# Attention as fp16 hi/lo products on four 64x64 tiles, and the graph phase's transposes and distances summed in PSUM

## The reference

```python
W = adj * adj
x = layernorm(x + einsum('bnf,nm->bmf', x, W) + bias)

z_l, z_g, v = x @ W_lang.T, x @ W_grav.T, x @ W_V.T
zn  = z_l / max(norm(z_l), 1e-8)
A_l = max(zn @ zn.T, 0) * not_eye
d2  = max(sq + sq.T - 2 * z_g @ z_g.T, 0)          # sq: squared norms of the rows of z_g
A_g = exp(-d2 / (2 * sigma**2)) * not_eye
K   = w * rownorm(A_l * adj) + (1 - w) * rownorm(A_g * adj)
x = layernorm(x + (K @ v) @ W_O.T)
```

## Time and profile before

| | before |
|---|---|
| median of 3 executions | 627.45 us (626.82 to 627.95) |
| span of the profiled execution | 625.0 us |
| TensorE busy | 614.2 us |
| vector engine busy | 444.2 us |
| ACT busy | 242.7 us |
| POOL busy | 155.5 us |

### The profile page before, as it was taken

How to read it: one execution, slowest core, us unless ns; L and a number is a source line. 1 busy time by engine, 2 the same in 40 slices (tenths; PEclk the granted TensorE clock), 3 DMA queues, 4 the chain that set the end, 5 groups by cost and what they waited for, 6 DMA issues and landing times.

```text
span 625.0 us, 11961 instructions
## 1 busy us (share of the span) xinstructions
PE 614.2 (98%) x4468; PEld 315.0 (50%) x4468; DVE 444.2 (71%) x940; ACT 242.7 (39%) x413; POOL 155.5 (25%) x159
## 2 busy tenths in 40 slices
PE   9999999999999999999999999999999999999994
PEld 6543545454454545454454545445454545545452
DVE  1759486877868586876868687786858788686564
ACT  2345224333443424434432433344342443443333
POOL 1002205032231403123230503223140312323021
PEclk9999999999999999999999999999999999999999
DMA  8722203434123342423223342312334242302103
GB/s 269 244 44 87 51 1 68 136 53 125 52 62 116 64 134 60 141 42 87 90 50 134 67 134 55 120 51 58 119 67 134 59 143 42 92 17 51 69 2 135
DMA packets 89392, 55.05 MB, mean 88 GB/s; under 512 B 70816, under 2 KB 70816, under 8 KB 89376
## 3 DMA queue, kind: packets, MB, share of 16 engines
q1 hardware_dynamic: 19744, 38.05, 17.9%
q10 hardware_dynamic: 69632, 16.79, 13.4%
HBM read 21.27 MB, written 16.78 MB: 61 GB/s over the span
## 4 chain that ended last, share of the span: by engine, by line
PE 96%; DVE 2%; ACT 1%; POOL 0%; issue 0%; POOLq 0%; ACTq 0%; DVEq 0%
PE proj L359 31%; PE proj L375 27%; PE front L339 9%; PE ps_t L389 7%; PE front L429 4%; PE ps_k L429 4%; PE ps_t L400 3%; PE ps_v L409 2%; PE proj L499 2%; PE proj L529 2%; PE ps_v L416 2%; PE ps_t L499 1%; PE ps_k L329 1%; DVE p_lo L736 1%; PE ps_t L529 1%; DVE y L709 0%
## 5 line engine op out<-in xcount | busy, mean ns | idle before, releaser
L557 ACT ACTIVATE p_hi<-proj 128x512 f16<-128x512 f32 x128 | 75.9, 593 | 118.2 <-PE proj L359 117.7
L736 DVE TENSOR_TENSOR p_lo<-proj,p_hi 128x512 f16<-128x512 f32 x128 | 86.0, 688 | 20.9 <-ACT p_hi L557 17.9
L375 PE MATMUL proj<-m_hi,ht_hi 128*128 128x512 f16 x256 | 97.2, 380 | 0.7 <-DVE p_lo L736 0.7
L375 PE MATMUL proj<-m_hi,ht_lo 128*128 128x512 f16 x256 | 97.0, 379 | 0.0
L375 PE MATMUL proj<-m_lo,ht_hi 128*128 128x512 f16 x256 | 97.0, 379 | 0.0
L1026 POOL TENSOR_TENSOR ve<-mv,eps_ln 128x4 f32<-128x4 f32 x31 | 6.6, 212 | 307.7 <-DVE mv L718 211.5
L562 ACT ACTIVATE u<-proj 128x512 f32<-128x512 f32 x64 | 37.9, 592 | 82.7 <-PE proj L375 82.5
L543 ACT ACTIVATE h_hi<-h 128x512 f16<-128x512 f32 x64 | 36.5, 619 | 69.0 <-DVE h L726 69.0
L1065 POOL TENSOR_TENSOR h_lo<-h,h_hi 128x512 f16<-128x512 f32 x30 | 41.5, 1403 | 84.4 <-ACT h_hi L543 84.4
L359 PE MATMUL proj<-ht_hi,l_grav_hi 128*128 128x512 f16 x160 | 60.6, 379 | 0.6 <-DVE p_lo L736 0.6
L359 PE MATMUL proj<-ht_hi,l_lang_hi 128*128 128x512 f16 x160 | 60.8, 380 | 0.0
(11 more groups left out here) (166 smaller groups left out, 1051.8 us busy)
## 6 DMA issues: line engine op xcount, KB each, us to landing
x_in<-in_x SPq DMA_DIRECT2D x16, 1024.0 KB, 7.1
out<-o SPq DMA_DIRECT2D x15, 1024.0 KB, 5.0
w_raw_lang<-in_L_gnn_W_lang SPq DMA_DIRECT2D x4, 256.0 KB, 3.1
o<-in_L_gnn_W_O SPq DMA_DIRECT2D x1, 1024.0 KB, 10.2
w_raw_grav<-in_L_gnn_W_grav SPq DMA_DIRECT2D x4, 256.0 KB, 10.1
u<-in_L_gnn_W_V SPq DMA_DIRECT2D x1, 1024.0 KB, 12.0
ht_hi<-h_hi ACTq DMA_TRANSPOSE x64, 2.4
ht_lo<-h_lo ACTq DMA_TRANSPOSE x64, 2.5
```

Of the source, the lines that this page charges most:

```text
L375: mm = pe.matmul(proj[j % 3][:, :], a[g.parity][:, k, p * P:(p + 1) * P], b[:, k, :], start=(n == 0), stop=(n == len(passes) - 1))
L557: act.activation(p_hi[:, j % 4, :, j // 4, :], by_batch(proj[j % 3]), ACT.Copy).then_inc(phi_ready, 1)
L736: dve.tensor_tensor(p_lo[:, j % 4, :, j // 4, :], by_batch(proj[j % 3]), p_hi[:, j % 4, :, j // 4, :], ALU.subtract).then_inc(plo_ready, 1)
```

## The change

- values(g, p) writes each output half with a 64-column product of its own, and takes batches in another order: output half q of value tile p holds batch rows from pair p // 2 * 2 + q, half p % 2.
- u and kt become fp16 hi and lo parts. ACT copies the hi part (u_high, kt_high), the vector engine subtracts for the lo part (u_low, kt_low). kt loses its zero blocks.
- attend is 12 products of 64 rows by 64 columns by 512 for each two pairs, so 24 in all; the wait for all of it stands ahead of the last product of project(g, 2). The fourth output goes to ps_t instead of ps_k.
- symmetrise adds T^T for the lang half alone, onto T in PSUM. The grav half's distances come out of spread and 8 transposes added on it in ps_v (r_sb, w_spread; the mask is part of w_spread, and the scale of T is gone from t_copy). The vector engine's sums and distances go, `shifted` comes; ACT gets `rectify`.
- residual becomes scalar_tensor_tensor with a scale; the last group's residual is scaled by ident_ku.

The diff at its core, first TensorE:

```diff
-            def project(g, j, first):
+            def project(g, j, first, attended=None):
...
-                        pe.wait_ge(u_ready, g.prev().count(4, j + 2))
+                        pe.wait_ge(ulo_ready, g.prev().count(4, j + 2))
...
                 for n, (k, a, b) in enumerate(passes):
+                    if attended and n == len(passes) - 1:
+                        attend_waits(*attended)
                     mm = pe.matmul(proj[j % 3][:, :], a[s][:, blk(k, c), :], b[g.parity][:, k, :],
...
             def values(g, p, first=False):
...
-                    mm = pe.matmul(proj[j % 3][:, :], a[g.parity][:, k, p * P:(p + 1) * P], b[:, k, :],
-                                   start=(n == 0), stop=(n == len(passes) - 1))
+                    for q in range(2):
+                        rows = (p // 2 * 2 + q) * P + p % 2 * N
+                        mm = pe.matmul(proj[j % 3][q * N:(q + 1) * N, :], a[g.parity][:, k, rows:rows + N], b[:, k, :],
+                                       start=(n == 0), stop=(n == len(passes) - 1))
...
             def symmetrise(g):
                 pe.wait_ge(t_ready, g.count(1, 1))
                 for b in range(GB):
-                    for half, eye in ((L, eye_l), (GR, eye_g)):
-                        mm = pe.matmul(ps_t[half, b * N:(b + 1) * N], t_sb[:, b * N:(b + 1) * N],
-                                       eye[:, :], start=True, stop=True)
+                    mm = pe.matmul(ps_t[L, b * N:(b + 1) * N], t_sb[:, b * N:(b + 1) * N],
+                                   eye_l[:, :], start=False, stop=True, skip_group_check=True)
...
             def spread(g, first):
-                pe.wait_ge(v_ready, g.count(1, 1))
+                pe.wait_ge(shifted_ready, g.count(1, 1))
+                pe.wait_ge(r_ready, g.count(1, 1))
...
-                pe.matmul(ps_v[:, :], ones_lg[:, :], v_diag[:, :], start=True, stop=True).then_inc(dj_done, 1)
+                pe.matmul(ps_v[:, :], w_spread[:, :], r_sb[:, :],
+                          start=True, stop=True, skip_group_check=True).then_inc(spread_done, 1)
+                for b in range(GB):
+                    mm = pe.matmul(ps_v[GR, b * N:(b + 1) * N], r_sb[:, b * N:(b + 1) * N],
+                                   eye_g[:, :], start=False, stop=True, skip_group_check=True)
+                mm.then_inc(d2_done, 1)
...
             def kernel_t(g):
-                    p, q = b // 2, b % 2
+                    p, q = b // 4 * 2 + b % 2, b // 2 % 2
...
+            def attend_waits(g, nxt):
+                pe.wait_ge(ktlo_ready, g.count(1, 1))
+                pe.wait_ge(ulo_ready, g.count(4, 4))
+                if nxt:
+                    pe.wait_ge(y_ready, nxt.count(4, 4))
+
+            def attend(g, a, banks, on_residual=()):
+                passes = ((kt_hi, u_hi), (kt_hi, u_lo), (kt_lo, u_hi))
+                for n, (kt, u) in enumerate(passes):
+                    for q in range(2):
+                        half = slice(q * N, (q + 1) * N)
+                        for side in range(2):
+                            mm = pe.matmul(banks[2 * a + q][side * N:(side + 1) * N, :], kt[half, 2 * a + side, :],
+                                           u[half, 2 * a + side, :], start=(n == 0 and 2 * a + q not in on_residual),
+                                           stop=(n == len(passes) - 1))
+                mm.then_inc(ku_done, 1)
...
-                project(g, 2, first)
+                project(g, 2, first, (before, nxt) if has_prev else None)
                 if has_prev:
-                    for p in range(PAIRS):
-                        attend(before, p, nxt)
+                    for a in range(2):
+                        attend(before, a, ku_bank)
...
+            pe.matmul(ps_v[L, 0:N], mask[:, :], eye_l[:, :], start=True, stop=True).then_inc(mask_turned, 1)
```

The vector engine (ACT's kt_high is one 128x256 copy for two of 64x256; POOL has one pow less):

```diff
+            def u_low(g, p):
+                dve.wait_ge(uhi_ready, g.count(4, p + 1))
+                dve.tensor_tensor(u_lo[:, p, :], proj[(8 + p) % 3][:, :], u_hi[:, p, :],
+                                  ALU.subtract).then_inc(ulo_ready, 1)
+
+            def kt_low(g):
+                dve.wait_ge(kthi_ready, g.count(1, 1))
+                dve.tensor_tensor(kt_lo[:, :, :], ps_v[:, 0:PAIRS * N].rearrange("p (a n) -> p a n", a=PAIRS),
+                                  kt_hi[:, :, :], ALU.subtract).then_inc(ktlo_ready, 1)
...
             def residual(g, p, first):
-                dve.wait_ge(ku_done, g.count(4, p + 1))
+                dve.wait_ge(ku_done, g.count(2, p // 2 + 1))
...
-                dve.tensor_tensor(o[:, p, :], ku_bank[p][:, :], h[g.parity][:, p, :], ALU.add).then_inc(sum_ready, 1)
+                dve.scalar_tensor_tensor(out=o[:, p, :], in0=ku_bank[p][:, :], scalar=ku_scale[:, 0:1],
+                                         in1=h[g.parity][:, p, :], op0=ALU.mult, op1=ALU.add).then_inc(sum_ready, 1)
...
             def back(g):
-                similarities(g)
+                u_low(g, 3)
                 gravities(g)
                 row_factors(g, None)
                 scale_rows(g)
+                kt_low(g)
...
             def iteration(g, has_prev, has_next):
...
                 if has_prev:
-                    similarities(before)
+                    u_low(before, 3)
                     gravities(before)
...
                 p_low(g, 1)
+                if has_prev:
+                    kt_low(before)
...
                     for p in range(PAIRS):
                         out_stats(before, p)
+                    if has_next:
+                        u_low(g, 0)
                     out_moments(before)
                     out_shift(before)
...
                 diagonals(g)
+                shifted(g)
+                if first or not has_next:
+                    u_low(g, 0)
+                u_low(g, 1)
                 diagonal_matrices(g)
-                sums(g)
-                distances(g)
+                similarities(g)
+                u_low(g, 2)
```

More of the change, by code:

```diff
@@ L391, in gram @@
                                        t[g.parity][:, c, b * N:(b + 1) * N],
-                                       start=(n == 0), stop=(n == len(passes) - 1))
+                                       start=(b == 0 and n == 0), stop=(n == len(passes) - 1),
+                                       skip_group_check=True)
                 mm.then_inc(gram_done, 1)
@@ L418, in kernel_t, with last_residual @@
                 mm.then_inc(kt_done, 1)
-            def attend(g, p, mixed):
-                if mixed and p in (1, 2):
-                    pe.wait_ge(y_ready, mixed.count(4, p + 2))
-                if p == 0:
[L425 to L431, removed]
+            def attend_waits(g, nxt):
[13 more added lines that the diff above has]
+                mm.then_inc(ku_done, 1)
+            def last_residual(g, p):
+                if p == 0:
+                    pe.wait_ge(last_ready, 2)
                 if p < 2:
@@ L617, in iteration @@
                 if has_prev:
-                    kt_copy(before)
+                    kt_high(before)
                 p_high(g, 2, first)
@@ L656, in iteration @@
                 if not has_next:
+                    rectify(g)
                     exponent(g)
-                u_copy(g, 2)
+                u_high(g, 2)
                 if has_prev:
@@ L661, in iteration @@
                 if has_next:
-                    exponent(g)
+                    rectify(g)
+                    exponent(g, first)
                 if has_prev:
                     normalise(before, (3,))
-                u_copy(g, 3)
+                u_high(g, 3)
             for k in range(DC):
@@ L770, in similarities @@
+                dve.wait_ge(rr_ready, g.count(1, 1))
+                dve.tensor_tensor(by_batch(r_sb, 0, N), over_batches(eye2, 0, N), over_columns(rr, 0, N),
+                                  ALU.mult).then_inc(r_ready, 1)
             def similarities(g):
-                dve.wait_ge(mr_ready, g.count(1, 1))
-                dve.scalar_tensor_tensor(out=a_sb[L, :], in0=s_sb[L, :], scalar=0.0, in1=w_sb[L, :],
-                                         op0=ALU.max, op1=ALU.mult).then_inc(a_ready, 1)
+                dve.wait_ge(relu_ready, g.count(1, 1))
@@ L799, in row_factors @@
                 dve.wait_ge(deg_ready, g.count(5, 4))
-                dve.scalar_tensor_tensor(out=cfac[:, :], in0=dinv[:, :], scalar=wv_scale[:, 0:1], in1=rr[:, :],
+                dve.scalar_tensor_tensor(out=cfac[:, :], in0=dinv[:, :], scalar=kt_scale[:, 0:1], in1=rr[:, :],
                                          op0=ALU.mult, op1=ALU.mult).then_inc(deg_ready, 1)
@@ L871, in back @@
                 dve.wait_ge(o_moved, g.prev().count(16, 32))
-                dve.wait_ge(ku_done, g.count(4, 4))
-                dve.tensor_tensor(o[:, 3, :], last_ku_bank[3][:, :], h[g.parity][:, 3, :], ALU.add).then_inc(sum_ready, 1)
+                dve.wait_ge(ku_done, g.count(2, 2))
```

(3 more changed lines are left out.)

178 lines of the change are left out of this document (89 added, 89 removed).

## The result

The changed kernel takes 660.23 us (median of 4 runs, 659.15 to 661.17) against 627.7 (4 runs, 626.82 to 628.09): 1.0521 times as long, interval 1.0506 to 1.0536. The profiled span is 657.8 us, at a mean granted clock of 0.994. Forecast were 660.3 and a span of 657.8.

A forecast was written before the change was run, and what follows sets the result against it. TensorE's instruction order was taken to bound the kernel. Span 625.0 + 24.6 (14 middle groups) + 2.5 (setup, group 0) + 5.7 (group 15, tail) = 657.8, plus 2.45 to the median: 660.3 us, range 648 to 672, chance 0.62.

The forecast's parts named there:

- TensorE's own need: TensorE's work in one middle group without waits: 35.4 us, a sum of changes of -0.30.
- rival A: In attend, row halves don't overlap, so it takes 12 slots: 670 us; chance 0.08.
- The changes of mode: Going into or out of 64-column tiles on TensorE: six a group at about 0.125 us, +0.50 a group.
- First stall: Before the sixth product of project(g, 2), TensorE waits for kt_low, delayed by u_low(before, 3): 0.92 us.
- Second stall: Before project(g, 6), TensorE waits for p_low(3), no longer covered by the longer attend: 1.10 us (0.86 to 1.5).
- Period: Length of one middle group, stalls included: 37.50 us, +1.76, times 14 groups.
- The ends: Setup and group 0 together +2.5 us; group 15 and the tail +5.7 us.
- The sum: Whole kernel: the span with middle groups and ends added, plus 2.45 from span to median: 660.3 us.
- B: In values, 64-column loads don't hide, so a pair costs 0.06 us more: 706 us; chance 0.05, unpaired case included.
- C: Middle groups have only the first stall: 645 us; chance 0.17, with the case between C and D.
- D: The u_low subtractions never reach TensorE's path, so both stalls and the ends' waits go: 624 us; chance 0.08.
- nothing is bought back: After the first stall all of TensorE is delayed, as the next group's start is counted from values 3 again.

The follow-up runs named there:

- e4: The kernel before with only its values made of pairs of 64-column products, all else as it was: 637.04 us, 1.0139.
- e12: Changed kernel with e7's tail, attend one projection later, and the Gram matrices' copy, diagonals and inverse norms taken earlier: 629.57 us, 1.0032.
- e2: Changed kernel with p_low(3) ahead of norm_rows and the copies of h, ScalarE's order to suit: 670.79 us, 1.0684.
- e8: e7 with p_high(3) first and both copies of h one step later on ScalarE and the vector engine: 654.36 us, 1.0424.
- e7: Changed kernel with gravities ahead of u_low(before, 3), and u_low(1), u_low(2), u_low(3) later in the last group and tail: 646.02 us, 1.0288.

## Why the prediction was right

- **TensorE's own need, 35.4 forecast**: 35.47. The attention came as priced, 1.51 us for 1.54, so row halves do overlap and rival A is out. The changes of mode did not: the way out of the column pairs took 0.23 before the spread and 0.29 behind values 3, where 0.125 stood. Against that symmetrise took 0.78 (333.97 to 334.75) for 0.93, and kernel_t 0.76 (350.37 to 351.13) for 0.84.
- **First stall, 0.92**: 0.85. Several errors of my terms met. The copy of values 3 starts 0.40 behind the product's slot, not 0.20, since column pairs carry a tail: in this trace a copy starts 0.21 behind pairs recorded 0.38 long, 0.35 behind 0.52 and 0.40 behind 0.58, as here. So gravities start at 343.76, 1.75 behind the slot, for the 1.43 of the text. Against that the vector engine needs 8.77 from there to kt_low (352.53), not 9.03, and TensorE arrives 10.22 behind the slot, not 10.02, through the slower way out of the values. It starts 0.14 behind kt_low's end (352.94), not 0.06. These are +0.32, -0.26, -0.20 and +0.08, which come to the difference of 0.07 within rounding.

```profile
341.79 0.58 PE L387 MATMUL proj<-m_hi,ht_lo 128*64 128x512 f16 x2
...
342.41 0.60 ACT L591 ACTIVATE uv<-proj 128x512 f16<-128x512 f32 x1 [1.07 <-PE proj L387]
```

- **Second stall, 1.10**: 0.97 by the bracket, 1.13 start to start (359.79 + 0.22 to 361.14). The residuals run at 0.66 from start to start, the value taken.
- **Period, 37.50**: 37.45, of which the stalls are 1.98 for the 2.02 forecast.
- **The ends, +8.2**: 32.8 - 23.9 = 8.9. Group 15's spread waits 2.06 for r, which stands behind u_low(1) (forecast 2.1), and in the tail gravities stand behind u_low(3), so that kernel_t waits 3.50 for ks:

```profile
631.75 0.69 DVE L769 TENSOR_TENSOR uv<-proj,uv 128x512 f16<-128x512 f32 x1 [2.62 <-ACT uv L591]
632.36 0.67 DVE L796 TENSOR_TENSOR r_sb<-eye,rr 64x512 f32<-64x512 f32 x1
...
633.14 1.10 PE L422 MATMUL ps_v<-r_sb,w_spread 128*128 128x512 f32 x2 [2.06 <-issue]
...
641.16 0.69 DVE L769 TENSOR_TENSOR uv<-proj,uv 128x512 f16<-128x512 f32 x1 [1.90 <-ACT uv L591]
641.88 0.69 DVE L808 SCALAR_TENSOR_TENSOR a_sb<-e_sb,mask 64x512 f32<-64x512 f32 x1
...
645.05 0.73 PE L434 MATMUL ps_v<-eye,ks_sb 128*64 128x64 f32 x16 [3.50 <-DVE ks_sb L835]
```

- **The sum, 660.3**: 660.23. The mechanism and its places are as written down, but the last 0.1 us is luck: the middle groups took 0.7 less than forecast and the ends 0.7 more. The 2.45 from span to median fitted as well (2.43), though the profiled execution itself took 659.64.
- **Rivals.** B fell by e4. By the Trainium skill ("TensorEngine Tiling (Array Packing)", Restrictions and Gotchas) column tiles lose the fast load; here no time shows for it. In the changed kernel the fp16 loads of 64 columns last 110 ns each (98 for 128 columns before), not the 138 that B was priced with. Two of them are 0.22, about one slot, so the unchanged step does not tell whether the two loads run side by side. C and D fell by the list of waits. D's 624 stood for no stall anywhere; that kernel could be built only by another order (e12), and takes 629.57.

What "nothing is bought back" hid: the two stalls and the order at the ends, 31 us, are a matter of order alone, on TensorE and in the queues that feed it (660.2 to 629.6 at the same arithmetic).

## What to carry to other kernels

Where one engine is busy in all of the span, a cheaper form of its work helps only if the copies that feed it have slack at the place where they are awaited; the shortened work was also their cover. Price the stall by walking the other engines' queues in order, and try to put the consumer one stage later before giving up the idea. Moving one copy alone to take its wait away can cost more than the wait (e2, e8): look at what stands behind it in every queue that it shares. And run the parts of a change apart: here one part was worth 2.1% and the other took it back.

## What the runs showed of the hardware

- Four 64x64 tiles run side by side: six steps of 0.22 for 24 fp16 products of 512 columns.
- A change between 128- and 64-column tiles costs about 0.15 us (e4: 0.62 for four). In the changed kernel the way out took 0.10, 0.23 and 0.29, behind column pairs recorded 0.38, 0.52 and 0.58 long.
- Two subtractions with operands in SBUF, on the vector engine and on GpSimd, lengthen the one that starts second: the vector engine's from 0.70 to 1.4 to 1.6 (e8, e2), or GpSimd's from 1.16 to 1.60 (the changed kernel). The low part of a projection, which reads PSUM, kept 0.69 beside it: in the changed kernel two of them take 1.29 from 361.63, while GpSimd's second copy of h runs.
- At the end TensorE idled for 3.5 us before the kernel's products, and its clock was granted at 0.50, the lower of its two levels (1.2 GHz), over the last attention; steps were 0.43 in place of 0.22. In e7, where TensorE does not idle ahead of kernel_t, the same products run at a granted 1.00 and 0.22 a step. The changed kernel:

```profile
646.70:649.10 2.40, 2.39 (x24) 0.93 (x24) 0.84 (x2) 0.00 (x0) 0.00 (x0) 0.50 0.00 0
```
